# Down projection of the routed experts: two of three chunks as three fp32r products of rounded halves, the results scaled on ScalarE

## What is computed

```python
def _moe(xf, gate_w, w1, w2, w3):          # 512 tokens x 512, 32 experts, 6 chosen for each token
    ...
    top_w, top_i = _gate(xf, gate_w)
    ...
    h = jax.nn.silu(jnp.einsum('ecd,edi->eci', xb, w1)) * jnp.einsum('ecd,edi->eci', xb, w3)
    ob = jnp.einsum('eci,eid->ecd', h, w2)   # w2: 32 x 352 x 512, the down projection
    ...
    y_pairs = ob[buf_idx] * w_s[:, None]
    y = jnp.zeros((T, D), xf.dtype).at[t_s].add(y_pairs)
```

## Time and profile before

| | |
|---|---|
| time, median of 3 runs (range) | 1038.76 us (1038.08 to 1039.44) |
| the profiled execution: its time, its span | 1036.27 us, 1034.5 us |
| PE, DVE, ACT, POOL busy | 988.1, 668.9, 541.1, 246.5 us |
| DMA | 144.00 MB, 139 GB/s over the span |
| the items: PE from about 757 to 1023 us | 36 items |

### The profile page before, as it was taken

How to read it: one execution, slowest core, us unless ns; L and a number is a source line. 1 busy time by engine, 2 the same in 40 slices (tenths; PEclk the granted TensorE clock), 3 DMA queues, 4 the chain that set the end, 5 groups by cost and what they waited for, 6 DMA issues and landing times.

```text
span 1034.5 us, 18651 instructions
## 1 busy us (share of the span) xinstructions
PE 988.1 (96%) x5440; PEld 826.4 (80%) x5441; DVE 668.9 (65%) x1014; ACT 541.1 (52%) x885; POOL 246.5 (24%) x170
## 2 busy tenths in 40 slices
PE   6899899999999978999999999979999999999997
PEld 5788698989988866888888887757878777778784
DVE  5655655676557735778766675746656767667765
ACT  5544575666666545455455552541345555555551
POOL 1300221222122130333333300010023343333331
PEclk9999999999999999999999999989999999999999
DMA  9100353321232331222122105310567898998995
GB/s 322 34 0 1 84 197 103 101 77 39 87 101 60 74 107 46 81 81 81 61 81 81 41 21 189 103 41 1 209 212 232 289 317 280 346 329 287 291 329 153
DMA packets 75277, 144.00 MB, mean 139 GB/s; under 512 B 13444, under 2 KB 40452, under 8 KB 74992
## 3 DMA queue, kind: packets, MB, share of 16 engines
q1 hardware_dynamic: 67392, 131.48, 37.6%
q0 software_dynamic: 7856, 12.16, 5.5%
HBM read 146.86 MB, written 14.02 MB: 156 GB/s over the span
## 4 chain that ended last, share of the span: by engine, by line
PE 80%; DVE 6%; DMA 5%; ACT 3%; issue 3%; SPq 2%; DVEq 0%; ACTq 0%
PE ps L316 19%; PE ps L317 19%; PE ps L318 19%; PE ps L874 8%; PE ps L670 6%; DMA w_raw<-in_w 3%; PE ps L736 1%; PE ps L746 1%; PE ps L729 1%; DMA w_and_lists<-in_w 1%; PE ps L917 1%; DMA wo_raw<-in_owT 1%; SPq L845 1%; PE ps L863 1%; PE ps L349 1%
## 5 line engine op out<-in xcount | busy, mean ns | idle before, releaser
L888 DVE TENSOR_TENSOR w_l<-w_raw,w_h 128x1408 fp32r<-128x1408 f32 x76 | 121.5, 1623 | 30.3 <-ACT w_h L884 20.8
L884 ACT ACTIVATE w_h<-w_raw 128x1408 fp32r (+1 forms) x76 | 102.5, 1372 | 40.2 <-DMA w_raw<-in_w 28.9
L874 PE MATMUL ps<-w_and_lists,hT 128*128 (+3 forms) x264 | 121.3, 595 | 0.0
L692 POOL TENSOR_TENSOR lw_l<-lw_raw,lw_h 128x1024 fp32r<-128x1024 f32 x32 | 77.1, 2415 | 146.4 <-ACT lw_h L688 145.9
L316 PE MATMUL ps<-w_h,xeT_h 128*128 x288 | 96.8, 336 | 2.6 <-DVE w_l L888 2.1
L317 PE MATMUL ps<-w_l,xeT_h 128*128 x288 | 93.0, 323 | 0.0
L318 PE MATMUL ps<-w_h,xeT_l 128*128 x288 | 92.9, 323 | 0.0
L990 POOL DMA_INDIRECT xe<-xn_scratch,take x37 | 39.5, 1069 | 222.8 <-DVE ob L957 143.8
L874 PEld LDWEIGHTS ps<-w_and_lists,hT 128*128 128x128 f32 (+1 forms) x264 | 48.1, 189 | 43.7 <-issue 43.1
L316 PE MATMUL ps<-xT_hi,lw_h 128*128 128x512 f32 x192 | 77.3, 402 | 0.0
L317 PE MATMUL ps<-xT_lo,lw_h 128*128 128x512 f32 x192 | 76.4, 398 | 0.0
(11 more groups left out here) (306 smaller groups left out, 2563.9 us busy)
## 6 DMA issues: line engine op xcount, KB each, us to landing
w_raw<-in_w SPq DMA_DIRECT2D x78, 704.0 KB
w_and_lists<-in_w SPq DMA_DIRECT2D x39, 512.0 KB
w_and_lists<-in_w SPq DMA_DIRECT2D x39, 192.0 KB
rkB<-rk_scratch SPq DMA_DIRECT2D x56, 128.0 KB, 3.2
wq_raw<-in_Wq SPq DMA_DIRECT2D x8, 512.0 KB, 4.8
wo_raw<-in_Wo SPq DMA_DIRECT2D x16, 256.0 KB, 2.8
lw_raw<-in_kwT SPq DMA_DIRECT2D x8, 512.0 KB, 3.4
lw_raw<-in_qwT SPq DMA_DIRECT2D x8, 512.0 KB, 3.3
```

The lines of the kernel that those rows point to most:

```text
L692: e.tensor_tensor(lw_l[n][:, :, :], lw_raw[n][:, :, :], lw_h[n][:, :, :], ALU.subtract).then_inc(lw_ready[n], 1)
L874: m = e.matmul(ps[:, 6 + k, :], hT[r, k, c, :], w2_raw[r, slot(w), c, :], start=c == 0, stop=c == FC - 1)
L884: e.activation(w13_h[:, k, n, :, :], w13_raw[:, slot(raw), n, :, :], ACT.Copy).then_inc(w13_hi_s, 1)
L888: e.tensor_tensor(w13_l[:, k, n, :, :], w13_raw[:, slot(raw), n, :, :], w13_h[:, k, n, :, :], ALU.subtract).then_inc(w13_ready, 1)
```

## The change

The down projections of the routed items take a new form on PE: the first two chunks are made with `mm3` from halves, the third (96 rows) stays fp32. The halves need four operations more for each item: ACT writes the high halves of hT (in place of the fp32 copy) and of two chunks of w2, DVE writes the low halves of both. The halves of w2 lie in `xT_hi` and `xT_lo`. The scaling of the results moves from DVE to ACT. `home` and `gateT` change their place in SBUF. SP issues the load of w1 and w3 of item 4 after those of w2 of items 1 to 3, not before. The first down projection of the loop, still of the shared expert, keeps its form.

```diff
+        def ex_down_halves(e, m, k, w):
+            e.wait_ge(hT_ready, m * 2 + (NSH + 2))
+            e.wait_ge(d_read, m + (NSH - 1))
+            e.wait_ge(w2_ready, m + 1)
+            for c in range(FC - 1):
+                mm3(ps[:, 6 + k, :], hT_h[:, k, c, :], hT_l[:, k, c, :], xT_hi[:, 2 * k + c, :], xT_lo[:, 2 * k + c, :],
+                    c == 0, False)
+            r = slice(0, FW[-1])
+            e.matmul(ps[:, 6 + k, :], hT[r, k, FC - 1, :], w2_raw[r, slot(w), FC - 1, :], start=False, stop=True).then_inc(d_ps, 1)
...
+        def ex_act_hT_halves(e, m, k):
+            e.wait_ge(hT_ps, m + (NSH + 1))
+            whole, r = (FC - 1) * P, slice(0, FW[-1])
+            e.activation(hT[r, k, FC - 1, :], ps[r, 5, whole:whole + P], ACT.Copy)
+            e.activation(hT_h[:, k, :, :].rearrange("p c n -> p (c n)"), ps[:, 5, 0:whole], ACT.Copy).then_inc(hT_ready, 1)
+        def ex_dve_hT_low(e, m, k):
+            e.wait_ge(hT_ready, m * 2 + (NSH + 1))
+            e.tensor_tensor(hT_l[:, k, :, :].rearrange("p c n -> p (c n)"), ps[:, 5, 0:(FC - 1) * P],
+                            hT_h[:, k, :, :].rearrange("p c n -> p (c n)"), ALU.subtract).then_inc(hT_ready, 1)
+        def ex_act_w2(e, i, k, raw):
+            e.wait_ge(w2_in[k], i * 32 + 64)
+            e.activation(xT_hi[:, 2 * k:2 * k + 2, :], w2_raw[:, slot(raw), 0:FC - 1, :], ACT.Copy).then_inc(w2_hi_s, 1)
+        def ex_dve_w2(e, m, k, raw):
+            e.wait_ge(w2_hi_s, m + 1)
+            e.tensor_tensor(xT_lo[:, 2 * k:2 * k + 2, :], w2_raw[:, slot(raw), 0:FC - 1, :], xT_hi[:, 2 * k:2 * k + 2, :],
+                            ALU.subtract).then_inc(w2_ready, 1)
+        def ex_act_ob(e, i, k):
+            m = i * 2 + k
+            if not isinstance(i, int) or i > 0:
+                e.wait_ge(acc_done[k], i * 16)
+            e.wait_ge(d_ps, m + (NSH + 1))
+            e.activation(ob[:, k, :], ps[:, 6 + k, :], ACT.Copy, scale=wl[:, bass.ds(m, 1)]).then_inc(d_read, 1)
...
-            ex_down(e, 1 - k, m + (NSH - 1), 1 if first else item_value(e, FIRST, m - 1, 3),
-                    (w2_in[1], 32) if first else (w2_in[1 - k], i * 32 + (k + 1) * 32), m + (NSH - 2))
-            ex_hT(e, k, m + NSH)
+            if first:
+                ex_down(e, 1, NSH - 1, 1, (w2_in[1], 32), NSH - 2)
+            else:
+                ex_down_halves(e, m - 1, 1 - k, item_value(e, FIRST, m - 1, 3))
+            ex_hT(e, k, m + NSH, m * 2 + NSH)
...
-            for m in (2, 3, 4):
+            for m in (2, 3):
                 ex_load_w13(e, m, m % 2, m // 2 + 1, values[m])
             for m in (1, 2, 3):
                 ex_load_w2(e, m, m % 2, m // 2 + 1, values[m])
+            ex_load_w13(e, 4, 0, 3, values[4])
...
+            ex_act_hT_halves(e, last_act * 2 + 1, 1)
+            for k in range(2):
+                ex_act_ob(e, last_act, k)
...
             ex_dve(e, last_i, 1, raw, ahead_i, last=True)
-            for k in range(2):
-                ex_dve_ob(e, last_i, k, give_away=False)
+            ex_dve_hT_low(e, last_i * 2 + 1, 1)
```

More of the change, by code:

```diff
@@ L195, in perceiver_block @@
         gw_l = sbuf(moe, "gw_l", [P, DC, E], F32R)
-        gateT = sbuf(moe, "gateT", [E, T])
+        with ExitStack() as router_rows:
+            gateT = sbuf(router_rows, "gateT", [E, T])
+        hT_l = sbuf(moe, "hT_l", [P, 2, FC - 1, P], F32R)
         gate = sbuf(moe, "gate", [P, TT, E])
@@ L310, in perceiver_block @@
         hT_ps, hT_ready, d_ps = sem("hT_ps"), sem("hT_ready"), sem("d_ps")
+        w2_hi_s, w2_ready = sem("w2_hi_s"), sem("w2_ready")
         steps = [0]
@@ L857, in ex_up, with ex_hT @@
                 m.then_inc(s, 1)
-        def ex_hT(e, k, u):
+        def ex_hT(e, k, u, read):
             e.wait_ge(h_ready, u + 1)
-            e.wait_ge(hT_ready, u)
+            e.wait_ge(hT_ready, read)
             for c in range(FC):
@@ L953, in ex_dve_ob @@
                 e.wait_ge(acc_done[k], i * 16)
[L954 to L957, removed]
+            e.tensor_copy(give[:, k:k + 1], tl[:, bass.ds(m, 1)]).then_inc(give_ready, 1)
         def ex_dve_x(e, u):
@@ L964, in ex_dve_x, with ex_dve @@
             e.tensor_tensor(x[:, u % TT, :], x[:, u % TT, :], ps[:, 6 + u % 2, :], ALU.add).then_inc(d_read, 1)
-        def ex_dve(e, i, k, ahead=None, last=False):
+        def ex_dve(e, i, k, own, ahead=None, last=False):
             m = i * 2 + k
[L969 to L974, removed]
+            if not isinstance(m, int) or m > 0:
+                ex_dve_hT_low(e, m - 1, 1 - k)
+            if not last:
+                ex_dve_xT(e, m + 1, 1 - k)
+                ex_dve_take(e, m + 3, 1 - k)
             if isinstance(i, int) and i == 0:
@@ L977, in ex_dve @@
             else:
-                ex_dve_ob(e, i - 1 if ahead is None else ahead, k)
+                ex_dve_give(e, i - 1 if ahead is None else ahead, k)
             ex_dve_h(e, k, m + NSH)
-            if not isinstance(m, int) or m > 0:
-                raw = raw_slot(e, m + 1)
+            raw = None if last else raw_slot(e, m + 1)
+            if not last and (not isinstance(m, int) or m > 0):
                 ex_dve_w13(e, 1 - k, 0, m * 2 + 7, raw)
                 ex_dve_w13(e, 1 - k, 1, m * 2 + 8, raw)
+            ex_dve_w2(e, m, k, own)
+            return raw
         def ex_dve_take(e, m, k):
@@ L1405, in _ @@
             ex_act_xT(e, 0, 0)
[L1406 to L1413, removed]
+            raw = ex_act(e, 0, 0, 0)
+            raw = ex_act(e, 0, 1, raw)
+            raw = ex_act(e, 1, 0, raw)
+            ex_act(e, 1, 1, raw)
+            with e.Fori(2, last_act) as i:
+                raw = ex_act(e, i, 0, raw_slot(e, i * 2))
+                ex_act(e, i, 1, raw)
+            ahead_act = turn_ahead(e)
+            raw = ex_act(e, last_act, 0, raw_slot(e, last_act * 2), ahead_act)
+            ex_act(e, last_act, 1, raw, ahead_act, last=True)
+            ex_act_hT_halves(e, last_act * 2 + 1, 1)
+            for k in range(2):
+                ex_act_ob(e, last_act, k)
         @block.vector
```

57 lines of the change are left out of this document (33 added, 24 removed).

## The result

The changed kernel takes 1028.79 us (median of 9 runs, 1025.51 to 1034.88) against 1038.66 us (9 runs, 1034.93 to 1041.84) for the kernel before on the same chip. The ratio is 0.9911, 95% interval 0.9887 to 0.9935, a gain of 6.8 to 11.7 us with 9.2 in the middle. The forecast was 1032.7 us, a gain of 6.1. Two later comparisons gave 0.9957 [0.9937, 0.9977] and 0.9924 [0.9897, 0.9951].

What follows compares the result with a forecast made beforehand. PE was taken to bound the items, except where weight loads set the pace. Gains of 4.9 + 1.05 + 0.15 = 6.1 us took 1038.76 to 1032.7 us; own range 1029.5 to 1035 (55%), 8 in 10 for 1027 to 1037.5.

Steps and rivals of the forecast that it cites:

- The product: PE's routed down projection: six fp32r matmuls at 0.2265 us replace four fp32 records, saving 0.35 to 0.37 us, 0.37 taken.
- The gain of a turn: PE's turn where PE sets the pace: from 7.24 us to 6.89, a gain of 0.35 us an item.
- second loop: PE's up projection waits for the low half of w1 after the shorter down projection, losing 0.02 to 0.03 us an item.
- PE stretches: Parts of the item loop where PE, not the weight loads, sets the pace, at 7.24 us an item before the change.
- 14 turns at 0.35: Turns 1 to 14, until item 16's w2 load is released: PE rules and 4.9 us are gained.
- Load stretches: 0: Turns where weight landings set the pace, 7.69 us an item to turn 25 and 50.5 us at the last: no gain.
- The rule weighed in the prediction: Weight loads at 425 GB/s would land an item in 6.2 us, leaving no load stretch; that rival had 8%.
- The waits priced at nothing: New or moved waits on ACT, SP and PE cost nothing; ACT's scaling behind the scatter at most 0.3 us in some items.
- The sum of DVE's turn: DVE's operations from h to h add up to 6.54 us, fitting in 6.89 with 0.35 to spare.
- before 862: Sign of being right: ACT's waits for DMA exceed 20.6 us and begin before 862 us.
- The end: After the last items: shorter down projection, later second-sum read and earlier adds give 0.15 us gain, between -0.8 and +1.4.

Runs made afterwards that it cites:

- a_own_slot: Changed kernel in which an expert's second item reads the converted w1 and w3 in its own slot, not the first item's; 1029.81 us, ratio 0.9898 to the kernel before.
- light loads: Kernel before and changed kernel, each with only two parts of w1 and w3 per load in the loop; 1031.64 us (0.9932) and 1024.68 us (0.9865).
- a_old_down: Changed kernel with all halves and the scaling on ACT, but the down projection in plain fp32; 1034.18 us, ratio 0.9969 to the kernel before.
- a_own_tail2: Second run of the changed kernel with own-slot weights and the last scatter's list made straight after the weight subtractions; 1028.56 us, ratio 0.9909 to the kernel before.
- b_light: Kernel before with only two of four chunks of w1 and w3 loaded from item 7 on; 1031.64 us, ratio 0.9932 to the kernel before.
- b_again: Kernel before, unchanged, run once more; ratio 1.0006 to the kernel before.
- b_pe_only: Kernel before with two chunks of each routed down projection as three fp32r matmuls, but no halves made; 1029.99 us, ratio 0.9936 to the kernel before.

## Why the prediction was right or wrong

The time, 1028.8, is on the right side. It lies under the forecast's own range (1029.5 to 1035) and inside the wider one given for 8 in 10 (1027 to 1037.5). The mechanism in the turns is the one forecast, but it is worth 3.9 us with the end, not 6.1, and by it alone the time would have been 1034.8. That the measured gain is over 6.1 and not under it comes from something that the prediction did not have. The terms:

**The product** was a little over-valued: 0.33 us shorter by the timeline (0.37 taken, from records 0.4335 apart, where the item's own 2.57 / 6 with 0.23 gives 0.35 or less), pace of 0.23 us.

**The gain of a turn** was 0.32 where I took 0.35, and the "second loop", by which I came from 0.37 to 0.35, isn't in the trace: in ordinary turns of the PE stretches PE doesn't wait for the low half of w1. It waits for it in the turns after an expert's second item and in the load stretches (the waits listed by place; 0.5 us at the most), so the 0.32 is the product's own.

**14 turns at 0.35** failed in its count. Items 2, 7 and 14 do not gain, so it is 11 x 0.32 = 3.5, measured 3.3. The trace of before showed it: DVE's idle time before w_l is 1.10 there, not 0.44, and PE's distance 3.66, not 3.31. I had read one ordinary turn and multiplied. a_own_slot shows the cause.

**Load stretches: 0.** Nearly right. T17 to T25 gave 0.3 us (2.3 with light loads) and the last stretch 0.7, where single profiles differ by more; turns 15 to 17, which I had counted to the first load stretch, gave 0.7, most of three turns' gain. The rule weighed in the prediction, 425 GB/s for a large load in the Trainium skill ("DMA: Bandwidth & Descriptors", section Bandwidth), isn't reached in this case: 336 and 340 GB/s at shares near 1 after and before, and 363 at the most in the slices of any page of the profiles. That figure is for one transfer of 16 MB, and the loads here are 704 KB each; for 1 MB the same table has 341 GB/s, which is what the trace shows.

**The waits priced at nothing** were right in the turns: with ACT's scaling behind the scatter's landing, with the scaling on either engine, and with the halves made but not used, ordinary turns stay at 6.92 or 7.24 us. The sum of DVE's turn, 6.54 us, was too high: in the trace `give` starts 6.16 us after h (780.89 to 787.05), and with the scaling behind it (0.74) a turn just fits in 6.92, where my sum would give 7.28. The records up to `give` I had summed nearly right (6.20); what was too much is 0.27 us for a semaphore behind them, and for the scaling the whole record of 0.74, which overlaps its neighbours. ACT does wait for more landings before 862 us (5.5 us in 6 places, forecast "before 862"), but PE's turns don't show it.

**The end** was mis-sized: +0.15 with bounds -0.8 and +1.4 was the forecast, a loss of 1.4 (1.2 to 1.6) the measurement, beyond the lower bound. The scatter's start, forecast 0.5 to 1 us later, was 1.0 later; missing was the scatter's own length, 1.0 us more. I had also read the earlier trace rows wrongly: the adds at 1026.86 show no wait, the second sum had landed 0.8 us earlier, so of the 2.1 us only the part beyond that cover counts. Where the scatter is not held up (a_old_down), the end is 15.6 us; there it starts 0.09 us ahead of a subtraction, here 0.06 us behind its start, so it was by chance that this cost came or not. In a_own_tail2 it was short as well (1.60 us) and started 3.58 us before T35, by then waiting for ACT's scaling, yet the second read went out 3.74 us after T35, only 0.3 to 0.5 earlier than in the changed kernel, and the end was 17.1: from the scatter's start to that read it is 7.3 us there, 5.4 to 5.8 in the changed kernel and 4.7 in the one before. Why so early a scatter takes longer to land isn't shown.

**What lies ahead of the items** was not forecast at all, and in the first pair of profiles it holds the rest of the gain. The first pair of profiles differs by 9.3 us in span, 4.7 in the items and 4.6 before them (first transposes of item 0 at 759.15 and 754.60). No instruction that matters was moved there; what differs most is the granted clock. Busy time by stretch, of the kernel before and then of the changed one:

```profile
683.00:689.00 6.00, 4.49 (x13) 1.82 (x12) 1.71 (x3) 1.05 (x2) 0.00 (x0) 0.50 0.34 127
```

```profile
683.00:689.00 6.00, 6.00 (x34) 4.77 (x33) 0.00 (x0) 3.34 (x4) 0.00 (x0) 1.00 0.00 0
```

Ahead of this PE waited 4.8 us for the normalization on DVE (in the kernel before, PE was busy 0.16 us of the 4 from 675 to 679 us, at a clock of 1.00). Then the clock stood at 0.50 (1.2 GHz) for 10.2 us in the kernel before and for 3.4 us in the changed one. From PE's transposes behind that wait to item 0 it is 76.7 to 77.0 us in the five profiles with 3.4 us at the lower level there, and 78.7 to 79.2 in the nine with 10.2: this is worth 2.1 us, about half of the 4.6. The other half stands ahead of it, since these transposes start at 679.99 us in the kernel before and at 677.57 in the changed one. There the kernel before has 3.4 us at the lower level from 41.0 us on, the changed one none (granted clock from 41 to 44 us 0.50 and 1.00). From one operation of DVE (`cT_l` at 19.61 and 18.87 us) to a later one (`ssk` at 58.70 and 56.43) it is 38.9 to 39.1 us in the nine profiles that have this stretch and 37.5 to 37.6 in the five that don't, which is 1.5 us. Another 0.7 us are lost ahead of the first of the two.

Each of these stretches shows in kernels made from the one before and from the changed one: the short stretch of 3.4 us behind the wait in b_light and four of the changed kind, the long one in before, b_again, b_pe_only and six of the changed kind. So the change alone doesn't set them. Item 0 starts at 758.6 us on average in the four profiles of the one kind and at 757.5 in the ten of the other, with a spread (standard deviation) near 2 us within each, so a small effect of the change ahead of the items is not excluded either. The timed runs say the same of the clock: a straight line through time and mean granted clock of each run, fitted over 163 runs with a level for each kernel and chip, gives 0.85 us for 0.001 of clock. At a clock of 0.990 the changed kernel then stands at 1030.4 and 1030.2 us in two comparisons and the kernel before at 1035.7, 1038.2 and 1037.9 (95% intervals of 0.7 to 1.4 us to either side). This takes out most of what differs between the runs of the changed kernel, and leaves two things open: why the kernel before is 2.4 us quicker on one chip than on the other two, and why a_old_down, which has the old product, stands at 1035.1, 2.8 us under the kernel before beside it. The items of their single profiles are within 1 us. That run keeps all other parts of the change, so part of the gain may belong to them. I can't say whether it is the order of the loads, the place of the tiles or the executions that the profiles didn't catch. So of the timed gain about 4 us are shown to be the product's (3.9 in the items with the end, and 4.2 between the medians of the changed kernel and a_old_down on one chip); the rest, from 0.5 to 5 us by the comparison, isn't explained by it.

## What to carry to other kernels

Before a saving is multiplied by a count, list the length of every turn in the trace: the turns that differ from the ordinary one by a wait are those in which another chain rules, and here 4 of the 17 turns in the PE stretches gained nothing. Added work on the engines beside the bound cost nothing here until the last item, where nothing covers it: sum the tail by itself, with every record on the chain that ends last. And a timed gain that is larger than the sum over the changed region is no confirmation of the sum: compare the unchanged region and its granted clock first.

## What the runs showed of the hardware

A scatter that GpSimd issues is held up by VectorE's subtractions in SBUF. Timelines of POOL and DVE, kernel before, the first where the scatter starts ahead of the pair of subtractions and the second where it starts inside:

```profile
794.23 1.58 POOL L994 DMA_INDIRECT y_scratch<-ob,give  x1 [0.30 <-issue]
...
845.82 2.81 POOL L994 DMA_INDIRECT y_scratch<-ob,give  x1 [0.30 <-issue]
```

```profile
794.49 3.16 DVE L888 TENSOR_TENSOR w_l<-w_raw,w_h 128x1408 fp32r<-128x1408 f32 x2 [0.43 <-issue]
...
845.53 3.16 DVE L888 TENSOR_TENSOR w_l<-w_raw,w_h 128x1408 fp32r<-128x1408 f32 x2 [0.42 <-issue]
```

And the changed kernel:

```profile
789.34 2.54 POOL L1047 DMA_INDIRECT y_scratch<-ob,give  x1 [0.31 <-issue]
...
796.30 1.59 POOL L1047 DMA_INDIRECT y_scratch<-ob,give  x1 [0.30 <-issue]
```

```profile
788.80 3.16 DVE L904 TENSOR_TENSOR w_l<-w_raw,w_h 128x1408 fp32r<-128x1408 f32 x2 [0.43 <-issue]
...
796.40 3.16 DVE L904 TENSOR_TENSOR w_l<-w_raw,w_h 128x1408 fp32r<-128x1408 f32 x2 [1.10 <-ACT w_h L900]
```

Each pair is two subtractions, the first over 1.54 us after the start. A scatter that starts 0.54 us into it is held for 1.00 and then takes its 1.55, together 2.55 (2.54 measured); one that starts 0.29 into it, 1.25 + 1.55 = 2.80 (2.81). So it waits for the instruction under way, not for the pair, as I had put it. One that starts first takes 1.59, and the subtractions behind it still take 3.16. The shorter down projection moved the gather and the scatter against VectorE's work, from just ahead of the pair to just inside: mean 2.39 us where it was 1.63, times 34 scatters, which is POOL's 26 us. At the end it starts 0.06 us into the low half of w2 (1006.15 and 1006.09) and takes 1.0 us longer. The Trainium skill ("SBUF — State Buffer", section "SBUF: two separate sides") says that VectorE with two inputs in SBUF and a GpSimd instruction that reads SBUF take a shared pair of ports as an exclusive lock for a whole instruction. The trace agrees for the scatter that comes second; that the one that comes first holds up VectorE isn't seen here: in the kernel before, subtractions of weights that start inside a scatter's record take 1.61 to 1.64 us, and the others 1.62 to 1.63.
